# A graph attention kernel: node projection ahead of edge counting, and 84 ring tiles gathered while the edges are counted

## Chip, cores and metric

The kernel runs on one core of one Trainium2 chip. The metric is the device time of one execution in microseconds. Before the change it is 3249.47 us, the median of 3 runs (3248.05 to 3252.27).

## What is computed

3125 nodes with 256 features and 50000 edges sorted by destination go through four layers, each added to its input: two graph attention layers, a mixture of experts, a five-hop graph convolution, and attention over slices. The change lies in the first stages of the graph layers. Of the reference that part is:

```python
hx = (x @ Wg).reshape(n, h, f)
he = (ea @ Wge).reshape(-1, h, f)
al = jax.nn.leaky_relu(einsum(hx, a_s)[src] + einsum(hx, a_d)[dst] + einsum(he, a_e), 0.2)
...
out = jax.ops.segment_sum(hx[src] * al[:, :, None], dst, num_segments=n)
```

Further on, the convolution sums `norm[:, None] * h[col]` over the edges five times. The kernel does that as a product with a dense matrix that holds, for each pair of nodes, how many edges join them. This matrix is what "counting the edges" means.

## The kernel before, in words

The edges are padded to 50176 and lie in 392 tiles of 128. The nodes are 25 blocks of 128. The program is a chain of stages. Each stage gives every engine its own list of instructions, and a barrier of all engines stands between two stages, so a stage ends when its last engine is done. The stages around the change are, in their order before:

- **Tables** (`graph_tables`): degrees, segment ends and the edge terms.
- **Counting** (`counts`, lines 944 to 1019, with the class `Counter`): 67 of the 131 windows of the count matrix. A window is three tiles of edges and one of overlap. Per window VectorE (DVE) writes a one-hot `dst_hot` (line 807) and three one-hots `src_hot` (line 812) in float16, TensorE (PE) multiplies them (line 845), ScalarE (ACT) copies the sum out (line 822) to one of three buffers, and SyncE (SP) stores it (line 830). After the windows DVE works out one "item" of a slow path for odd graphs (`AnyOrder`, lines 898 to 920). GpSimd (POOL) stores this item with an indirect DMA (line 928). It first waits for the semaphore `ready`, loads the number of items into a register (line 876), enters a loop, and waits for the item itself.
- **Projection** (`project_nodes`): `hx = x @ Wg` and the node terms, block by block, stored as rows of 260 floats in the DRAM tensor `hx_rows` (line 419).
- **Lookup** (`lookup`, lines 659 to 773): for each edge the source's terms, through one-hots and PE products. DVE multiplies by a mask (line 749) and reduces (line 733), 98 groups of four tiles. In each of the 14 chunks of seven groups it also makes one wide one-hot (line 725) and one mask (line 727).
- **Edge weights** (`edge_weights`): segment sums and maxima with scans, and 32 more counting windows beside them.
- **Aggregation** (`aggregate`): the rows gathered per edge are weighted and summed per node.

The rows per edge come from `Gather.on_gpsimd` (line 637): POOL issues one indirect DMA (line 645) per tile of 128 edges, which reads 128 rows of `hx_rows` into one slot of a ring of 112 tiles in SBUF. A counter of pairs of tiles says how far it may run ahead. In the first layer `AHEAD` is 56 pairs everywhere, so all 112 tiles of the ring are gathered in the lookup, and the next 280 wait in the aggregation until a slot is free. In the second layer 34 pairs are gathered in the lookup, and the rest of the ring in the edge weights.

The instructions of POOL stand in one queue per stage. In the lookup they are an iota (line 704), the clearing of the edge table (line 706), and then the gathers.

Of the kernel before, what the change touches and what calls it, by code (L numbers as in the profile page):

```python
# [43 lines left out]
def after(count):  # L44


    return count + 1


class Linked:  # L50


    def __init__(self, eng, sem, base=0):
        self.eng, self.sem, self.base, self.n = eng, sem, base, 0
# [7 lines left out]
class Space:  # L62
# [20 lines left out]
    def sb(self, name, shape, dt=F32):  # L83
        return self.ctx.enter_context(self.nc.sbuf_tensor(f"{self.tag}_{name}", shape, dt))
# [20 lines left out]
def across(row, width):  # L105

    return row.rearrange("(a n) -> a n", a=1).to_broadcast([P, width])
# [514 lines left out]
class Gather:  # L622

    AHEAD = ((56, 56, 56, 56), (34, 42, 46, 56))

    def __init__(self, nc, ctx, g, layer):
        s = Space(nc, ctx, f"gat{layer}")
        self.g, self.sent = g, 0  # L630
        self.upto = self.AHEAD[layer]
        self.ring = s.sb("ring", [P, RING, ROW])
# [311 lines left out]
def counts(nc, g, io):  # L944

    with ExitStack() as ctx:
        s = Space(nc, ctx, "cnt1")
        c = g.counter
        anyhow = AnyOrder(s, g)
        part, keys, lasts, numbers = (s.sb(n, [P, ET]) for n in ("part", "keys", "lasts", "numbers"))  # L950
        last_i = s.sb("last_i", [P, ET], I32)
        wide, long = s.sb("wide", [P, WINDOWS]), s.sb("long", [P, WINDOWS - 1])
        whole = [s.ps(f"acc{i}", (P, c.BANKS, 512)) for i in range(3)]
        apart = s.ps("apart", (P, c.BANKS, 512))
        numbered, linked, ready, given = (s.sem(n) for n in ("numbered", "linked", "ready", "given"))
        windows = range(c.MAIN)
        full = WINDOWS - 1
        with s.block() as block:
            @block.sync
            def _(sp):  # L960
                sp.dma_start(last_i[:, :], across(io["tile_last"], ET)).then_inc(given, 16)
                for j in windows:
                    c.store(sp, j)
                c.all_stored(sp, c.MAIN)

            @block.gpsimd
            def _(pool):
                pool.iota(c.number[:, :], pattern=[[1, QUARTER]], base=0, channel_multiplier=0,
                          allow_small_or_imprecise_dtypes=True).then_inc(numbered, 1)
                pool.iota(numbers[:, :], pattern=[[1, ET]], base=0, channel_multiplier=0,  # L970
                          allow_small_or_imprecise_dtypes=True).then_inc(numbered, 1)
                pool.iota(anyhow.lane[:, :], pattern=[[0, 1]], base=0, channel_multiplier=1).then_inc(numbered, 1)
                pool.wait_ge(ready, after(1))
                anyhow.on_gpsimd(pool)

            @block.vector
            def _(dve):
                link = Linked(dve, linked)
                column = c.column[:, :]
                link(dve.tensor_copy(c.count16[:, :], g.count[:, :]))  # L980
                link(dve.tensor_copy(column, g.src_i[:, :]))
                link(dve.tensor_scalar(part[:, :], column, float(QUARTER), None, ALU.is_ge))
                for q in (2, 3):
                    link(dve.scalar_tensor_tensor(part[:, :], column, float(q * QUARTER), part[:, :], ALU.is_ge, ALU.add))
                link(dve.scalar_tensor_tensor(column, part[:, :], float(-QUARTER), column, ALU.mult, ALU.add))
                link(dve.scalar_tensor_tensor(keys[:, :], g.dst_f[:, :], 4.0, part[:, :], ALU.mult, ALU.add))
                dve.wait_ge(given, after(16))
                link(dve.tensor_copy(lasts[:, :], last_i[:, :]))
                link(dve.memset(g.first4[:, 0:1], 0.0))
                link(dve.tensor_scalar(g.first4[:, 1:WINDOWS], lasts[:, TRIPLE - 1:ET - 1:TRIPLE], 4.0, 4.0, ALU.mult, ALU.add))  # L990
                link(dve.memset(g.first4[:, WINDOWS:], 4.0 * (N + 2)))
                base = g.first4[:, 0:full]
                link(dve.tensor_tensor(c.key[:, 0:full, 0:TRIPLE], keys[:, 0:TRIPLE * full].rearrange("p (j i) -> p j i", i=TRIPLE),
                                       base.unsqueeze(2).to_broadcast([P, full, TRIPLE]), ALU.subtract))
                link(dve.tensor_tensor(c.key[:, 0:full, TRIPLE], keys[:, TRIPLE:ET:TRIPLE], base, ALU.subtract))
                link(dve.tensor_tensor(c.key[:, full, 0:ET - TRIPLE * full], keys[:, TRIPLE * full:],
                                       g.first4[:, full:full + 1].to_broadcast([P, ET - TRIPLE * full]), ALU.subtract))
                dve.wait_ge(numbered, after(3))
                c.on_vector(dve, windows)
                link(dve.tensor_tensor(wide[:, :], g.first4[:, 1:], g.first4[:, 0:WINDOWS], ALU.subtract))  # L1000
                link(dve.tensor_scalar(wide[:, :], wide[:, :], float(4 * SPAN), None, ALU.is_gt))
                link(dve.tensor_tensor(long[:, :], lasts[:, TRIPLE:ET:TRIPLE], lasts[:, TRIPLE - 1:ET - 1:TRIPLE], ALU.is_equal))
                link(dve.tensor_tensor(wide[:, 0:full], wide[:, 0:full], long[:, :], ALU.add))
                link(dve.tensor_reduce(g.odd[:, :], wide[:, :], AX, ALU.max))
                link(dve.tensor_scalar(g.odd[:, :], g.odd[:, :], 1.0, None, ALU.min))
                link(dve.tensor_scalar(anyhow.items[:, :], g.odd[:, :], float(anyhow.ITEMS - 1), 1.0, ALU.mult, ALU.add))
                link(dve.memset(lasts[:, ET - 1:ET], float(NP - 1)))
                dve.sem_inc(ready, 1)
                anyhow.on_vector(dve, link, c, numbers, keys, lasts, apart)

            @block.scalar
            def _(act):
                c.on_scalar(act, windows, whole, False)

            @block.tensor
            def _(pe):
                c.on_tensor(pe, windows, whole)
                pe.wait_ge(ready, after(1))
                anyhow.on_tensor(pe, apart)
# [1462 lines left out]
def main_program(nc, io, out):  # L2482
    with ExitStack() as whole:
        g = Space(nc, whole, "all")
# [18 lines left out]
        with ExitStack() as graph:  # L2503
            sb = lambda n, shape, dt=F32: graph.enter_context(nc.sbuf_tensor(n, shape, dt))
            g.src_i, g.dst_f = sb("src_i", [P, ET], I32), sb("dst_f", [P, ET])
            g.indeg, g.inv_deg, g.has = (sb(n, [P, NB]) for n in ("indeg", "inv_deg", "has"))
            g.seg_start, g.seg_end = sb("seg_start", [P, NB], I32), sb("seg_end", [P, NB], I32)
            g.tiles, g.tile_quads = sb("tiles", [P, NB + 1], I32), sb("tile_quads", [P, NB + 1], I32)
            g.small_sb = sb("small_sb", [P, NB, SW])
            g.block_first = sb("block_first", [P, NB])  # L2510
            g.node_d, g.w_self = sb("node_d", [P, NB, 4]), sb("w_self", [P, NB, 4])
            graph_tables(nc, g, io)
            g.counter = Counter(nc, graph, g)
            counts(nc, g, io)
            project_nodes(nc, g, io, 0, io["x"], True)
            for layer, target in enumerate((g.x_mid, g.x_gnn)):
                if layer:
                    project_nodes(nc, g, io, layer, g.x_mid, False)
                with ExitStack() as held:

                    words = ET * SW + 2 * NB * SW
                    room = held.enter_context(nc.sbuf_tensor(f"room{layer}", [P, words], F32))
                    g.per_edge = room[:, 0:ET * SW].rearrange("p (j c) -> p j c", c=SW)
                    g.spare = room[:, ET * SW:ET * SW + 2 * NB * SW].rearrange("p (n b c) -> p n b c", n=2, c=SW)
                    g.gather = Gather(nc, held, g, layer)
                    lookup(nc, g, layer)
                    g.w_cols = held.enter_context(nc.sbuf_tensor(f"w_cols{layer}", [P, ET, 4], F32))
                    edge_weights(nc, g, io, layer)
                    aggregate(nc, g, io, layer, target)
# [40 lines left out]
```

## Time and profile before

| what | value |
|---|---|
| median of 3 runs | 3249.47 us |
| the profiled execution's own time | 3252.93 us |
| its span | 3251.1 us |
| counting, 153.5 to 288.7 us of the span | 135.2 us |
| projection, 288.7 to 362.9 us | 74.2 us |
| lookup, 362.9 to 531.4 us | 168.5 us |
| busy in the span: PE, DVE, ACT, POOL | 70%, 55%, 29%, 33% |

The stage bounds are the first instruction of a stage on any engine, read from the timeline. The busy shares are means over all stages and say nothing on a single one. In each stage the question is which engine reaches the barrier last. A timeline row gives the start, the length, the engine, the line and the operation, with the idle time ahead of it and what released it in brackets. Neighbouring instructions of one kind are merged into one row with their count.

### The profile page before, as it was taken

The page shows a single profiled execution, that of the slowest core. Times are in us where ns is not written, and L with a number is a line of the kernel's source. Part 1 is how long each engine was busy: PE and PEld are TensorE (multiplying, and loading weights), DVE is VectorE, ACT ScalarE, POOL GpSimd, SP SyncE. Part 2 cuts the span into 40 slices and gives each one's busy share as a digit, 9 for nine tenths or more (in the row PEclk, how much of TensorE's full clock was granted, in tenths as well). Part 3 has the DMA queues.
Part 4 walks back from the last instruction along what each step waited for, and adds up shares of the span by engine and source line. Part 5 has one row for each costly group of instructions (what it writes and reads, how often), then busy time and mean ns, then how long its engine had stood idle before and what let it go on. Part 6 is the DMA issues. An engine that isn't in the chain of part 4 may idle for free. (4 is left out here: it accounts for less than half of the span.)

```text
span 3251.1 us, 40675 instructions
## 1 busy us (share of the span) xinstructions
PE 2271.6 (70%) x11685; PEld 1667.0 (51%) x11685; DVE 1777.6 (55%) x4118; ACT 941.5 (29%) x1613; POOL 1056.9 (33%) x1034
## 2 busy tenths in 40 slices
PE   5394662628766554537887489915999999996767
PEld 1142452216544343215565367704888888884446
DVE  6497698657744357637775310058444444435643
ACT  5352100301100010210000012217666666662321
POOL 0000472717777526757777433030000000000000
PEclk9797886859987876769998689957999999998987
DMA  4133552324444345435555489343555565640001
GB/s 168 15 124 115 179 179 68 99 68 117 122 115 113 103 169 177 129 104 157 161 165 155 130 303 379 139 129 91 142 151 143 144 150 142 152 112 10 0 14 42
DMA packets 367972, 420.74 MB, mean 129 GB/s; under 512 B 47984, under 2 KB 325585, under 8 KB 364599
## 3 DMA queue, kind: packets, MB, share of 16 engines
q1 hardware_dynamic: 271530, 220.90, 22.8%
q0 software_dynamic: 50496, 151.73, 16.2%
q10 hardware_dynamic: 45792, 46.27, 4.3%
q8 instruction: 72, 1.18, 0.2%
q14 instruction: 82, 0.66, 0.1%
HBM read 329.39 MB, written 90.23 MB: 129 GB/s over the span
## 5 line engine op out<-in xcount | busy, mean ns | idle before, releaser
L645 POOL DMA_INDIRECT gat_ring<-hx_rows,src_i x784 | 820.4, 1046 | 335.8 <-issue 233.4
L2150 PE MATMUL hop_sums<-hop_pieces,hop_weights 128*128 128x512 f32 x3125 | 712.6, 390 | 107.4 <-DVE hop_pieces L2053 107.4
L2150 PEld LDWEIGHTS hop_sums<-hop_pieces,hop_weights 128*128 128x128 f32 x3125 | 588.7, 188 | 231.3 <-DVE hop_pieces L2053 109.1
L2088 ACT ACTIVATE hop_weights<-hop_columns 128x640 fp32r<-128x640 f16 x625 | 459.8, 739 | 221.5 <-PE hop_sums L2150 207.5
L1614 PE MATMUL agg_acc<-agg_msg,agg_oh 128*128 x976 | 275.5, 434 | 120.7 <-DVE agg_oh L1526 120.5
L1614 PE MATMUL agg_acc<-gat_ring,agg_oh 128*128 x976 | 261.7, 411 | 71.0 <-DVE agg_oh L1523 68.5
L1614 PEld LDWEIGHTS agg_acc<-agg_msg,agg_oh 128*128 128x128 f32 x976 | 197.1, 212 | 194.5 <-issue 161.7
L1614 PEld LDWEIGHTS agg_acc<-gat_ring,agg_oh 128*128 128x128 f32 x976 | 178.0, 198 | 149.8 <-issue 129.8
L2203 POOL IOTA slc_valid<- 128x25 f32 x1 | 0.2, 163 | 757.3 <-POOLq L76 757.3
L1523 DVE TENSOR_SCALAR agg_oh<-agg_nodes,dst_f,w_cols 128x128 f32<-128x128 f32 x488 | 174.8, 405 | 121.6 <-PE agg_acc L1614 61.1
L770 PE MATMUL look_bank<-look_pieces,look_part 128*128 128x125 bf16 (+1 forms) x2352 | 149.1, 232 | 101.6 <-DVE look_part L725 52.3
L1509 DVE TENSOR_TENSOR agg_msg<-gat_ring,w_cols (+1 forms) x98 | 121.7, 1242 | 131.7 <-SPq L656 109.1
L770 PEld LDWEIGHTS look_bank<-look_pieces,look_part 128*128 128x128 f16 x2352 | 131.1, 114 | 120.0 <-DVE look_part L749 57.2
L2067 DVE TENSOR_SCALAR hop_h<-hop_sums,all_dis 128x256 f32<-128x256 f32 x125 | 60.5, 484 | 230.7 <-PE hop_sums L2150 230.5
L822 ACT ACTIVATE cnt_out<-wts_acc 128x800 f16<-128x800 f32 x64 | 53.6, 837 | 398.3 <-PE wts_acc L845 395.2
L812 DVE TENSOR_SCALAR cnt_src_hot<-cnt_number,cnt_column 128x800 f16<-128x800 f16 x392 | 144.3, 420 | 1.9 <-PE wts_acc L845 1.5
L845 PE MATMUL wts_acc<-cnt_src_hot,cnt_dst_hot 128*128 128x400 f16 x508 | 101.4, 353 | 59.9 <-DVE cnt_src_hot L812 56.4
L845 PE MATMUL cnt_acc<-cnt_src_hot,cnt_dst_hot 128*128 128x400 f16 x536 | 103.2, 338 | 47.8 <-DVE cnt_src_hot L812 42.6
L1871 DVE TENSOR_TENSOR exp_y<-exp_down,exp_b 128x256 f32<-128x256 f32 x32 | 11.3, 416 | 225.2 <-PE exp_down L1922 225.2
L1908 PE MATMUL exp_up<-exp_xt,exp_w 128*128 128x512 f32 x256 | 124.2, 613 | 6.6 <-ACT exp_xt L1881 6.6
L1922 PE MATMUL exp_down<-exp_w,exp_hid 128*128 128x256 f32 x512 | 119.6, 379 | 0.0
L1526 DVE TENSOR_TENSOR agg_oh<-agg_nodes,dst_f 128x256 f32<-128x256 f32 x244 | 96.5, 419 | 38.7 <-PE agg_acc L1614 35.0
(447 smaller groups left out, 3029.9 us busy)
## 6 DMA issues: line engine op xcount, KB each, us to landing
hop_columns<-count_rows SPq DMA_DIRECT2D x60, 1600.0 KB, 8.0
look_part<-src_low SPq DMA_DIRECT2D x28, 896.0 KB, 5.3
exp_w<-in_L_ffn_w SPq DMA_DIRECT2D x16, 1024.0 KB, 15.5
count_windows<-cnt_out SPq DMA_DIRECT2D x67, 200.0 KB, 1.9
count_windows<-cnt_out ACTq DMA_DIRECT2D x64, 200.0 KB, 1.9
gat_ring<-hx_rows,src_i POOLq DMA_INDIRECT x784, 2.8
hx_rows<-prj_row SPq DMA_DIRECT2D x50, 130.0 KB, 1.9
agg_own<-hx_rows ACTq DMA_DIRECT2D x50, 130.0 KB, 2.6
```

Source lines behind the costliest of these rows:

```text
L645: pool.indirect_dma_start(out=self.ring[:, t % RING, :], out_offset=None, in_=self.g.hx_rows, in_offset=bass.IndirectOffsetOnAxis(ap=self. ...
L770: mm = pe.matmul(bank[n % BANKS][:, k * WIDE:(k + 1) * WIDE], hot[c % 2][:, j * P:(j + 1) * P], pieces[:, piece, :], start=(piece == 0), s ...
L812: made = dve.tensor_scalar(self.src_hot[:, t % self.SRC, :], self.number[:, :], self.column[:, t:t + 1], None, ALU.is_equal)
L845: mm = pe.matmul(whole[j % sets][:, n, 0:self.COLS], self.dst_hot[:, j % self.HOT, i, :], self.src_hot[:, t % self.SRC, n * self.COLS:(n + ...
L1509: weighted = dve.tensor_tensor(at(msg, q % 2).rearrange("p (k f) -> p k f", f=F + 1), at(ring, q % HELD).rearrange("p (k f) -> p k f", f=F ...
L1523: hot = dve.tensor_scalar(oh[k][:, n, :], nodes[b % 2], at(g.dst_f, tile), at(g.w_cols, tile)[:, 0:1], ALU.is_equal, ALU.mult)
L1526: hot = dve.tensor_tensor(oh[k][:, :, :], nodes[b % 2].unsqueeze(1).to_broadcast([P, 2, P]), g.dst_f[:, bass.ds(4 * q + 2 * k, 2)].unsquee ...
L1614: mm = pe.matmul(sums, oh[k][:, n, :], moving[:, t:t + R], start=False, stop=False, skip_group_check=True)
L1908: mm = pe.matmul(up[c % 2][:, :], w1[i][:, k, c:FF:KF], xt[:, k, :], start=(k == 0), stop=(k == 1))
L1922: mm = pe.matmul(down[q][:, 0:D], hid[c % 2][:, q * P:(q + 1) * P], w2[i][:, c, :], start=(c == 0), stop=(c == KF - 1), skip_group_check=True)
L2088: act.activation(weights[:, q % SLOTS_W, :, :], columns[n % STAGES][:, c * GROUP:(c + 1) * GROUP, b % 2 * P:(b % 2 + 1) * P], ACT.Copy).th ...
L2150: mm = pe.matmul(sums[m % BANKS][:, :], weights[:, q % SLOTS_W, i, :], pieces[k % 2][:, t, :], start=(t == 0), stop=(t == NB - 1))
```

## The change

The call of `counts` moves behind the projection of the first layer, to a place where the ring exists. In it, POOL gathers 42 pairs, which are 84 of the ring's 112 tiles, after its three iotas and ahead of its wait for `ready`. The lookup then asks for 56 pairs as before, so that 28 tiles are left to it. Nothing else is edited.

```diff
     AHEAD = ((56, 56, 56, 56), (34, 42, 46, 56))
+    WHILE_COUNTING = 42
...
                 pool.iota(anyhow.lane[:, :], pattern=[[0, 1]], base=0, channel_multiplier=1).then_inc(numbered, 1)
+                g.gather.on_gpsimd(pool, g.gather.WHILE_COUNTING)
                 pool.wait_ge(ready, after(1))
                 anyhow.on_gpsimd(pool)
...
             g.counter = Counter(nc, graph, g)
-            counts(nc, g, io)
             project_nodes(nc, g, io, 0, io["x"], True)
...
                     g.gather = Gather(nc, held, g, layer)
+                    if not layer:
+                        counts(nc, g, io)
                     lookup(nc, g, layer)
```

On POOL, counting and lookup before (`cnt_...` are counting's tiles, `gat_ring` is the ring, `room` holds the edge table; TENSOR_LOAD is the load of the number of items, and the DMA to `count_rows` the store of the item):

```order
L968 IOTA cnt_number 128x800
L970 IOTA cnt_numbers 128x392
L972 IOTA cnt_lane 128x1
L876 TENSOR_LOAD cnt_items
L928 DMA count_rows<-cnt_item_out,cnt_item_rows 12800x800
L704 IOTA look_lane 128x1
L706 MEMSET room 128x3136
L645 DMA gat_ring<-hx_rows,src_i 128x260 x112
```

And now:

```order
L969 IOTA cnt_number 128x800
L971 IOTA cnt_numbers 128x392
L973 IOTA cnt_lane 128x1
L646 DMA gat_ring<-hx_rows,src_i 128x260 x84
L877 TENSOR_LOAD cnt_items
L929 DMA count_rows<-cnt_item_out,cnt_item_rows 12800x800
L705 IOTA look_lane 128x1
L707 MEMSET room 128x3136
L646 DMA gat_ring<-hx_rows,src_i 128x260 x28
```

84 gathers stand ahead of the load of the item count and of the item's store. 28 of the 112 stay where they were.

On SP's queue, from counting to the lookup before (`prj_x` and `prj_w` are the projection's input and weights, `look_part` the lookup's):

```order
L961 DMA cnt_last_i<-in_tile_last 128x392
L830 DMA count_windows<-cnt_out 128x800 x67
L311 DMA prj_x<-in_x 128x5x256 x5
L409 DMA prj_w<-in_L_gnn_Wg 128x2x256
L695 DMA look_part<-src_high 128x392
L699 DMA look_part<-src_low 128x3584 x14
```

And now:

```order
L311 DMA prj_x<-in_x 128x5x256 x5
L409 DMA prj_w<-in_L_gnn_Wg 128x2x256
L962 DMA cnt_last_i<-in_tile_last 128x392
L831 DMA count_windows<-cnt_out 128x800 x67
L696 DMA look_part<-src_high 128x392
L700 DMA look_part<-src_low 128x3584 x14
```

The two stages have changed places, and each has the same transfers as before.

## Rows read from the trace of the kernel before

**Rows 1.** Windows: stretches inside counting, its end, the projection's end, the lookup, its end.

```profile
core 0: us, PE busy (x) PEld busy (x) DVE busy (x) ACT busy (x) POOL busy (x), PEclk, DMA share, GB/s
200.00:220.00 20.00, 18.94 (x102) 8.78 (x100) 20.00 (x51) 10.51 (x13) 0.00 (x0) 1.00 0.34 128
340.00:363.00 23.00, 14.17 (x62) 9.26 (x60) 9.08 (x35) 5.27 (x12) 0.02 (x1) 0.94 0.38 127
372.00:516.00 144.00, 96.87 (x1122) 81.71 (x1119) 133.54 (x203) 0.00 (x0) 111.10 (x109) 0.80 0.56 176
```

**Rows 2.** Timeline of POOL: first, an ordinary and last of the lookup's 112 gathers.

```profile
366.04 0.99 POOL L645 DMA_INDIRECT gat_ring<-hx_rows,src_i  x1 [0.16 <-issue]
...
376.39 0.94 POOL L645 DMA_INDIRECT gat_ring<-hx_rows,src_i  x1 [0.30 <-issue]
377.64 0.94 POOL L645 DMA_INDIRECT gat_ring<-hx_rows,src_i  x1 [0.30 <-issue]
...
515.14 0.95 POOL L645 DMA_INDIRECT gat_ring<-hx_rows,src_i  x1 [0.30 <-issue]
```

**Rows 3.** Timeline of DVE: lookup groups beside gathers, after them, and the last one.

```profile
504.50 0.68 DVE L749 TENSOR_TENSOR look_part<-look_bank,look_part 128x500 f32<-128x500 f32 x1
...
505.89 0.68 DVE L749 TENSOR_TENSOR look_part<-look_bank,look_part 128x500 f32<-128x500 f32 x1
...
518.67 0.68 DVE L749 TENSOR_TENSOR look_part<-look_bank,look_part 128x500 f32<-128x500 f32 x1
...
520.07 0.68 DVE L749 TENSOR_TENSOR look_part<-look_bank,look_part 128x500 f32<-128x500 f32 x1
...
527.63 1.25 DVE L733 TENSOR_REDUCE room<-look_part 128x20 f32<-128x500 f32 x2
```

**Rows 4.** Timeline of counting: POOL's last iota, first window, and what follows the last window.

```profile
154.78 0.30 POOL L972 IOTA cnt_lane<- 128x1 int32 x1
...
160.09 0.69 DVE L807 TENSOR_TENSOR cnt_dst_hot<-cnt_count,cnt_key 128x512 f16<-128x512 f16 x1
...
268.99 0.28 DVE L1000 TENSOR_TENSOR cnt_wide<-all_first 128x131 f32<-128x131 f32 x1
```

**Rows 5.** Timeline of DVE: two neighbouring windows of counting, POOL idle.

```profile
201.16 0.68 DVE L807 TENSOR_TENSOR cnt_dst_hot<-cnt_count,cnt_key 128x512 f16<-128x512 f16 x1
201.76 1.10 DVE L812 TENSOR_SCALAR cnt_src_hot<-cnt_number,cnt_column 128x800 f16<-128x800 f16 x3
202.77 0.68 DVE L807 TENSOR_TENSOR cnt_dst_hot<-cnt_count,cnt_key 128x512 f16<-128x512 f16 x1
```

**Rows 6.** Timeline of POOL, second layer's edge weights: indirect DMAs while DVE makes counting windows.

```profile
1316.86 1.41 POOL L645 DMA_INDIRECT gat_ring<-hx_rows,src_i  x1 [0.30 <-issue]
1318.57 1.31 POOL L645 DMA_INDIRECT gat_ring<-hx_rows,src_i  x1 [0.30 <-issue]
1320.19 1.30 POOL L645 DMA_INDIRECT gat_ring<-hx_rows,src_i  x1 [0.30 <-issue]
1321.80 1.46 POOL L645 DMA_INDIRECT gat_ring<-hx_rows,src_i  x1 [0.30 <-issue]
...
1324.82 0.98 POOL L1156 DMA_INDIRECT room<-edge_scan,seg_end  x1 [0.30 <-issue]
1326.11 0.98 POOL L1156 DMA_INDIRECT room<-edge_scan,seg_end  x1 [0.30 <-issue]
```

**Rows 7.** Timeline of DVE at that place: two windows beside POOL's indirect DMAs.

```profile
1330.43 0.68 DVE L807 TENSOR_TENSOR cnt_dst_hot<-cnt_count,cnt_key 128x512 f16<-128x512 f16 x1
...
1332.04 0.68 DVE L807 TENSOR_TENSOR cnt_dst_hot<-cnt_count,cnt_key 128x512 f16<-128x512 f16 x1
```

**Rows 8.** Timeline of the end of counting, up to the next stage's first instruction.

```profile
273.04 0.72 DVE L887 MEMSET cnt_total<- 128x800 f32 x1 [0.23 <-DVE cnt_own L886]
274.87 0.42 DVE L898 TENSOR_SCALAR cnt_pick<-cnt_numbers,cnt_tile 128x392 f32<-128x392 f32 x1 [1.10 <-issue]
...
281.69 0.16 DVE L914 SCALAR_TENSOR_TENSOR cnt_item_rows<-cnt_window,cnt_row 128x1 int32<-128x1 f32 x1
...
282.77 1.15 POOL L928 DMA_INDIRECT count_rows<-cnt_item_out,cnt_item_rows  x1 [127.69 <-DVE cnt_item_rows L914]
288.76 4.42 SPq L311 DMA_DIRECT2D prj_x<-in_x  x5
```

**Rows 9.** Instructions on the tile cnt_out in counting: ACT's copies, SP's stores, landing.

```profile
L822 ACT ACTIVATE cnt_out<-cnt_acc x67: 837/837/838, 165.1 to 270.7; 128x800 f16<-128x800 f32 x67
L830 SPq DMA_DIRECT2D count_windows<-cnt_out x67: 319/320/342, 165.9 to 271.6; - x67
...
DMA to landing us min/median/max: 1.9/1.9/2.6
```

**Rows 10.** Instructions of line 645 in the lookup: the landing of its gathers.

```profile
DMA to landing us min/median/max: 2.7/2.8/6.1
```

## The prediction

> **What bounds the kernel now.** The stages are cut apart by barriers, so I read each touched stage for the engine that arrives last, and only then the change.
>
> First the windows by stage [rows 1]. In a stretch inside counting DVE is busy for all of its 20.00 us and POOL for none. In the lookup DVE is busy 133.54 of 144 us and POOL 111.10. In the projection's last stretch neither is full. So DVE is the suspect in counting and in the lookup, and POOL a second one in the lookup.
>
> Second, the lookup's timeline, to see who comes last. POOL's first gather starts at 366.04 and its 112th ends at 515.14 + 0.95 = 516.1 [rows 2]. DVE's last reduction ends at 527.63 + 1.25 = 528.9 [rows 3]. The gathers are therefore over 12.8 us before the stage is. They are also not in DVE's way: one group takes 505.89 - 504.50 = 1.39 us beside gathers and 520.07 - 518.67 = 1.40 us after the last one [rows 3]. The 112 gathers cost this stage nothing that I can see.
>
> Third, the end of counting. DVE's last window is done at 268.99 [rows 4]. The item's arithmetic follows; POOL, which has waited 127.69 us, issues the item's store at 282.77, 0.92 us after DVE's step at 281.69 + 0.16, and the next stage's first transfer is issued at 288.76 [rows 8]. SP's last store was issued at 271.6 and lands in 2.6 us at most [rows 9]. So POOL's store ends this stage: whatever delays POOL at 282.77 delays the program.
>
> **The change part by part.** *The swap of stages.* Projection and counting use nothing of each other. Each keeps its instructions and transfers, and each still begins with PE idle. I cost the swap at nothing; a microsecond either way at the boundaries goes into the range.
>
> *84 gathers out of the lookup.* They take 84 x (0.94 + 0.30) us off POOL there, and none off the stage, since DVE ends it and its beat is the same with and without them [rows 3]. I cost this at 0. If the cover were gone, that is if POOL ended the stage, the gain would be at most the time that DVE doesn't need, and here that is below zero. Nothing downstream gains either: the aggregation finds the ring full in both kernels, and its 280 further gathers wait for freed slots.
>
> *84 gathers into counting.* POOL is idle there, but the gathers stand ahead of the item's store in the same queue. So the question is whether 84 of them end before 281.85, when DVE hands the item over.
>
> Their pace is not the lookup's. Alone a gather starts every 1.25 us (377.64 - 376.39, [rows 2]). While DVE makes counting windows, four gathers started at 1316.86, 1318.57, 1320.19 and 1321.80, and took 1.30 to 1.46 us in place of 0.94 [rows 6]: mostly 1.61 us from start to start. That is the beat of the windows themselves, 202.77 - 201.16 = 1.61 us [rows 5]: one gather for each window. DVE pays nothing for it. Its window is 1332.04 - 1330.43 = 1.61 us beside POOL as well [rows 7].
>
> Here a page bears on it, and it speaks against this change. The Trainium skill, "SBUF — State Buffer", section "SBUF: two separate sides", says that DVE and GpSimd have one port pair in common, which whoever starts first holds for the whole instruction, and that a DMA issued from GpSimd can't have its descriptors written while a DVE instruction in a fast mode holds it. By that a gather would get on only in the windows' other part. The rows agree that POOL is held up beside these windows, and show no DVE instruction held up by a gather; the rule taken to its end is a rival below.
>
> Now the sum, on the profile's own clock.
> - POOL's last iota ends at 154.78 + 0.30 = 155.08 [rows 4]; with the 0.16 us ahead of the lookup's first gather [rows 2] the first starts at 155.24. Four start before the first window at 160.09 (155.24 + 3 x 1.25 = 158.99).
> - The fifth starts at 160.24. From there to 268.99 is 108.75 us, or 67.3 beats of 1.615. That gives 68 starts, the last at 268.45. Now 72 are issued, and POOL is free about 270.0 (1.31 + 0.30 later).
> - 12 are left, at 1.25 us: 15.0 us, the last one over at 284.7. In this stretch DVE still runs a few float16 and float32 one-hots and copies, such as the 0.72 and 0.42 us in [rows 8]; I add 1 us for them: 285.7.
> - Then POOL loads the item count and enters its loop. Before, this lay under its wait. DVE's own load and entry show as 1.10 us between 273.76 and 274.87 [rows 8]; POOL's I take as the same, and the 0.92 us up to the store as before. The store is issued at 285.7 + 1.1 + 0.9 = 287.7.
> - It was issued at 282.77. Late by 4.9 us, call it **+5 us**, all on the path, since the next stage follows this store.
>
> The bounds. Below: if no gather were held up, 84 x 1.25 = 105 us would end at 260.2, before the item is ready, and the change would cost 0. Above: if the beat of 1.615 held through the tail too, 84 x 1.615 = 135.7 us would end at 290.9, and the store would start at 292.9: +10. I take the middle case because the rows nearest to it, gathers of this very line beside these very windows, show one per window, and after the windows such instructions return to 0.94 us.
>
> The profiled execution took 3252.93 us, 3.5 above the median. 3252.93 + 5.0 - 3.5 = **3254.5 us**: 0.15% slower, inside the 0.2% (6.5 us) that a measurement of this kernel can tell from no change.
>
> **The rivals.**
>
> *POOL is in time.* The lock to the beat is not strict: at 1324.82 and 1326.11 two indirect DMAs passed in 0.98 us each, beside windows [rows 6], after DVE had paused. If every third gather goes like that, the 68 starts in the windows become some 75, four more gathers (5 us) are saved and the item is waited for again: +0 to +2 us, **3250.5 us**. For it: those rows. Against: [rows 6] also shows the beat taken up at once. Chance 0.18.
>
> *POOL is later.* The DVE work after the windows holds up gathers as the windows do, and the tail runs at 1.615: +10 us, **3259.5 us**. It decides from +6.5 us on, that is from a tail pace of about 1.4 us. For it: the item's arithmetic has such instructions. Against: they fill a small part of those 13 us. Chance 0.17.
>
> *The stores become the wait.* Stores already take 0.34 of the DMA engines in counting [rows 1]. Gathers of 133 KB each 1.61 us come on top. ACT copies into three buffers, so a buffer must come back within three beats, 4.84 us: 0.84 for the copy, 0.32 for the issue, and the landing, 1.9 us now [rows 9]. From a landing of about 3.6 us on, ACT, then PE, then DVE wait; each further microsecond costs 67 / 3 = 22 us. At 4.6 us: **3272 us**. For it: gathers in the lookup took up to 6.1 us to land [rows 10]. Against: the lookup moved 176 GB/s at a share of 0.56 [rows 1], and such landings were single ones. Chance 0.06.
>
> *The port is held to the end.* If a gather's 0.94 us had to fit into the 0.6 us of a window that is not `src_hot`, each would need two windows, 3.2 us. By 269 only 4 + 34 would be issued, 46 would be left, 57.5 us, the store at about 329: +46 us, **3296 us**. That is what the page's rule would give, taken strictly. Against: [rows 6] has one per window. Chance 0.03.
>
> *The lookup gains.* Faster needs DVE or its loads in the lookup to be slowed by gathers in a way that the beat of [rows 3] doesn't show. To pass 0.2% it must be 6.5 us, over 0.06 us on each of 98 groups, where I see 0.01. Price at that point: **3243 us**. Chance 0.06.
>
> **How the numbers follow.** The forecast, POOL late by 2 to 6.5 us, has 0.50; with "in time" (0.18) the same within 0.2% is 0.68. Slower is "later", "stores" and "port": 0.17 + 0.06 + 0.03 = 0.26. Faster is 0.06. The range of 8 in 10 takes in the three cases that differ by POOL's pace alone: from 0 less a boundary's 2 us to +10 and 1.5 us of scatter: 3247.5 to 3261.
>
> **What the changed profile would show.** The lookup as long as before, 166 to 169 us from its first instruction to the next stage's, with DVE's groups at 1.39 us, and POOL there done after 28 gathers. In counting, gathers of about 1.31 us, one per window; windows at 1.61 us; 70 to 74 gathers begun when the windows end; the item's store some 18 to 19 us after that in place of 13.8, and released by no wait for DVE. A store that still follows DVE's step by 0.92 us would show POOL in time. Windows longer than 1.61 us, with ACT waiting for landings, would show the stores. I would be wrong on the main point if counting and projection together grew by nothing while the lookup got shorter.

## The result, and the profile after

| | median us | runs | range us |
|---|---|---|---|
| before | 3252.08 | 10 | 3247.57 to 3255.57 |
| after | 3258.66 | 10 | 3255.62 to 3261.38 |

The ratio is 1.0023, with a 95% interval of 1.0013 to 1.0033. The change costs 6.6 us between the medians: slower, clear of no change, and at about the 0.2% that I had set as the line. The profiled execution after has a span of 3259.3 us (before 3251.1).

In the changed kernel the projection runs from 153.6 to 227.87 us of the span, counting to 370.60, and the lookup to 538.14. So the projection takes 74.2 us as before, counting 142.7 in place of 135.2, and the lookup 167.5 in place of 168.5. The two changed stages give +7.5 and -1.0, together +6.5, which is the difference of the medians. The two profiled executions differ by 8.2 us; the other 1.5 us lie behind the lookup, where the kernels are the same.

Windows of the changed kernel: inside counting, inside the lookup, and between the two (columns as in [rows 1]).

```profile
274.00:294.00 20.00, 18.95 (x102) 8.75 (x101) 20.00 (x51) 10.41 (x13) 16.35 (x13) 1.00 0.68 209
380.00:524.00 144.00, 97.97 (x1123) 82.99 (x1122) 133.50 (x203) 0.00 (x0) 23.76 (x24) 0.80 0.27 96
...
361.50:370.50 9.00, 0.00 (x0) 0.00 (x0) 0.00 (x0) 0.00 (x0) 0.00 (x0) 0.50 0.00 0
```

The first two answer to [rows 1]. In counting POOL is now busy for 16.35 of 20 us, and DVE makes the same 51 instructions in the same time. In the lookup POOL is almost empty, and DVE is as busy as before: 133.50 us. The third line is new. For 9 us no engine computes and no DMA engine moves a byte.

The timeline of POOL in the changed kernel: the first gather, two in step with the windows, the last two of that kind and the first after, the last, the item's store, and the lookup's first instruction.

```profile
229.39 1.11 POOL L646 DMA_INDIRECT gat_ring<-hx_rows,src_i  x1
...
242.94 1.31 POOL L646 DMA_INDIRECT gat_ring<-hx_rows,src_i  x1 [0.30 <-issue]
244.55 1.31 POOL L646 DMA_INDIRECT gat_ring<-hx_rows,src_i  x1 [0.30 <-issue]
...
343.08 1.31 POOL L646 DMA_INDIRECT gat_ring<-hx_rows,src_i  x1 [0.30 <-issue]
344.70 0.95 POOL L646 DMA_INDIRECT gat_ring<-hx_rows,src_i  x1 [0.30 <-issue]
...
357.84 0.95 POOL L646 DMA_INDIRECT gat_ring<-hx_rows,src_i  x1 [0.30 <-DVE cnt_item_rows L915]
359.09 1.01 POOL L929 DMA_INDIRECT count_rows<-cnt_item_out,cnt_item_rows  x1 [0.30 <-issue]
370.63 0.14 POOL L705 IOTA look_lane<- 128x1 f32 x1 [10.52 <-ACTq L693]
```

The gathers go as [rows 6] had them, one per window. The item's store follows the last gather at once. (The bracket of the last gather names DVE's item. In POOL's list that wait stands behind the gathers and ahead of the store, so the gather itself did not need it.) Then POOL seems to do nothing for 10.52 us.

The timeline of DVE in the changed kernel: two windows, the first step behind the windows, the hand-over of the item, counting's last step, the lookup's first, two groups of the lookup beside gathers, and its end.

```profile
273.44 0.67 DVE L808 TENSOR_TENSOR cnt_dst_hot<-cnt_count,cnt_key 128x512 f16<-128x512 f16 x1
...
275.06 0.67 DVE L808 TENSOR_TENSOR cnt_dst_hot<-cnt_count,cnt_key 128x512 f16<-128x512 f16 x1
...
344.50 0.28 DVE L1002 TENSOR_TENSOR cnt_wide<-all_first 128x131 f32<-128x131 f32 x1
...
357.45 0.16 DVE L915 SCALAR_TENSOR_TENSOR cnt_item_rows<-cnt_window,cnt_row 128x1 int32<-128x1 f32 x1
...
358.28 0.16 DVE L921 TENSOR_TENSOR cnt_tile<-cnt_tile,cnt_keep 128x1 f32<-128x1 f32 x1
370.64 0.25 DVE L713 COPY look_value<-small_sb 128x100 f32<-128x100 f32 x1 [12.20 <-PEq L76]
...
401.89 0.67 DVE L750 TENSOR_TENSOR look_part<-look_bank,look_part 128x500 f32<-128x500 f32 x1
...
403.28 0.68 DVE L750 TENSOR_TENSOR look_part<-look_bank,look_part 128x500 f32<-128x500 f32 x1
...
534.48 1.25 DVE L734 TENSOR_REDUCE room<-look_part 128x20 f32<-128x500 f32 x2
```

A window still takes 1.62 us [rows 5, 7] and a group of the lookup 1.39 [rows 3]. DVE is done with counting at 358.44 and then waits 12.20 us for the barrier.

What POOL does in that time is not among the busy instructions. It stands in its queue, under the line of the stage's block, where each engine issues a DRAIN ahead of the barrier. A row gives the length in ns (least, median, greatest) and the start. Counting's block in the changed kernel:

```profile
L959 DVEq DRAIN  x1: 17/17/17, 358.7 to 358.7; - x1
L959 POOLq DRAIN  x1: 7000/7000/7000, 362.0 to 362.0; - x1
```

The same in the kernel before:

```profile
L958 DVEq DRAIN  x1: 10/10/10, 282.9 to 282.9; - x1
L958 POOLq DRAIN  x1: 136/136/136, 285.8 to 285.8; - x1
```

POOL's drain has grown from 0.136 to 7.000 us, and it is the last thing ahead of the barrier. Before, the gathers had this drain in the lookup, where DVE came later. The lookup's block before (two layers; the first starts are the first layer's):

```profile
L692 POOLq DRAIN  x2: 20602/22870/25139, 500.2 to 1276.5; - x2
...
L692 DVEq DRAIN  x2: 10/10/10, 529.1 to 1281.0; - x2
```

In the first layer POOL's drain ended at 500.2 + 25.1 = 525.3, which is 9.2 us after the last gather's end at 516.1 [rows 2], and still 3.8 us ahead of DVE at 529.1. (POOL's queue runs ahead of the recorded spans, so a drain's row can begin while gathers are still running, as here at 500.2; its end is what counts.) In the second layer, where 68 gathers stand in the lookup, the same line has POOL's drain ending at 1276.5 + 20.6 = 1297.1, 16 us after DVE's at 1281.0. There gathers and drain end the stage already in the kernel before.

### The profile page after: what moved, and what is told of

Its sections match the earlier page's. It is cut to its first block and busy times, and to the rows that moved or that the text cites. A ratio compares the mean times of both kernels' runs of the same rounds, so it can differ in the third digit from the quotient of the medians.

```text
span 3259.3 us, 40667 instructions
## 1 busy us (share of the span) xinstructions
PE 2277.5 (70%) x11685; PEld 1672.3 (51%) x11685; DVE 1779.8 (55%) x4118; ACT 941.6 (29%) x1613; POOL 1077.1 (33%) x1034
## 5 line engine op out<-in xcount | busy, mean ns | idle before, releaser
L646 POOL DMA_INDIRECT gat_ring<-hx_rows,src_i x784 | 841.0, 1073 | 334.8 <-issue 231.1
```

The source lines that it names most:

```text
L646: pool.indirect_dma_start(out=self.ring[:, t % RING, :], out_offset=None, in_=self.g.hx_rows, in_offset=bass.IndirectOffsetOnAxis(ap=self. ...
```

## The experiments

The theories. **Order**: the swap of the stages costs the time, by its boundaries. **Backlog**: the drain waits for what the last gathers left behind; it goes if POOL has time between them and the block's end. **Fixed**: the drain costs a set time for each indirect DMA, whatever POOL waits for in between. I held the second to be likeliest.

### The swap alone (e1)

```diff
-    WHILE_COUNTING = 42
+    WHILE_COUNTING = 0
```

> The swap of the two stages alone: no tile is gathered while edges are counted, all 112 in the lookup. Theory 'backlog' (POOL's drain at the end of a stage waits for work of the indirect DMAs that no row shows as busy; it took 7.0 us in counting after the change and 0.14 us before): the drain is 0.1 to 0.3 us again, the item is stored 129 us after counting's first instruction as before, and the time is that of the kernel before within 1.5 us. Theory 'order' (the extra time lies in going from counting straight to the lookup): still 5 to 7 us slower than before.

Measured: 3251.11 us beside 3252.02 of before, ratio 0.9997 (0.9988 to 1.0007). The drain is back at its old length:

```profile
L959 POOLq DRAIN  x1: 136/136/136, 360.3 to 360.3; - x1
```

The swap is neutral. "Order" falls, and all of the cost is the gathers'.

### 72 tiles in place of 84 (e2)

```diff
-    WHILE_COUNTING = 42
+    WHILE_COUNTING = 36
```

> 36 pairs (72 tiles) in place of 42 while edges are counted; the last gather should end about 115 to 116 us after counting's first instruction, some 14 us before the item is handed over. 'Backlog': those 14 us are enough to work off a backlog of 8 to 9 us, the drain is under 1 us, and the time is from 0.5 us below to 2.5 us above the kernel before (what DVE lost in the stage, 1.5 us, may stay). 'Order': 5 to 7 us slower. 'Fixed' (a stage with gathers ends in a drain of some 0.08 us per gather, whenever they were issued): the drain is about 6 us and the time 5 to 7 us above the kernel before.

Measured: 3256.47 us, ratio 1.0016 (1.0007 to 1.0025). POOL's item store and the drain in this kernel, from the timeline and from the block's line:

```profile
358.49 1.01 POOL L929 DMA_INDIRECT count_rows<-cnt_item_out,cnt_item_rows  x1 [15.44 <-DVE cnt_item_rows L915]
```

```profile
L959 POOLq DRAIN  x1: 6020/6020/6020, 361.4 to 361.4; - x1
```

POOL now stood idle for 15.44 us before the item, so that it is late for nothing. The drain is 6.02 us all the same. What the gathers had left behind would have been gone in 15 us: "backlog" falls, and with it the theory that I had begun with.

### The item made late (e3)

84 tiles, and 13 more clearings of a buffer on DVE ahead of the item, each chained to the last:

```diff
-        link(dve.memset(self.total[:, :, :], 0.0))
+        for _ in range(14):
+            link(dve.memset(self.total[:, :, :], 0.0))
```

> The changed kernel with 13 more clearings of one tile on DVE, about 10 to 11 us, between the windows and the item; POOL's list is untouched. 'Backlog': the item is stored some 10 to 11 us later, but the drain behind it falls from 7.0 us to under 1 us, so the kernel is only 3 to 5 us slower than the changed one (10 to 12 us above the kernel before). 'Fixed': the drain stays at 7 us and the whole delay is paid: 10 to 11 us slower than the changed kernel (17 us above the kernel before).

Measured: 3270.14 us, ratio 1.0056 (1.004 to 1.0071). POOL waits 12.53 us for the item, and the drain does not shrink:

```profile
L960 POOLq DRAIN  x1: 7000/7000/7000, 373.7 to 373.7; - x1
```

It is the same 7.000 us with a wait ahead of it and without. That is "fixed", to the nanosecond.

### All 112 tiles while counting (e4)

```diff
-    WHILE_COUNTING = 42
+    WHILE_COUNTING = 56
```

> All 112 tiles while edges are counted, none in the lookup. By every theory the item waits for 28 more gathers at 1.25 us, 35 us, and the stage pays them: 40 to 46 us above the kernel before. 'Backlog': the drain is 8 to 11 us, as at the end of a run of 112 gathers in the lookup before (9.2 us from the last row to the end of the drain). The lookup now runs without a gather: by my prediction it takes 167 to 168.5 us as ever; if gathers slowed it, by the rival, it would be 3 us or more shorter.

Measured: 3297.76 us, ratio 1.0143 (1.0128 to 1.0159). POOL is late by its whole surplus: the item's store starts at 393.43, 36.6 us behind the start of DVE's hand-over at 356.80. The drain:

```profile
L959 POOLq DRAIN  x1: 9287/9287/9287, 396.4 to 396.4; - x1
```

0, 72, 84 and 112 gathers give 0.136, 6.020, 7.000 and 9.287 us. Each of the three is 0.136 + 0.0817 for every gather. And the lookup without a single gather beside it takes 165.2 us from its first instruction to its barrier, where with all 112 it takes 165.7 (e1) and 166.3 (the kernel before). The gathers cost DVE there about a microsecond at most, in its wait for the low halves (`src_low`): 0.5 us here, 1.3 in e1 and 1.8 before.

### 72 tiles, drained early (e5)

If the drain counts the indirect DMAs since the last drain, one more drain under POOL's 15 us wait must take the cost off the path:

```diff
                 g.gather.on_gpsimd(pool, g.gather.WHILE_COUNTING)
+                pool.drain()
                 pool.wait_ge(ready, after(1))
```

> As with 72 tiles, plus one explicit drain of POOL right behind the gathers of counting, ahead of its wait for the item. The drains measured so far are 0.136 us for the item alone, 6.020 for 72 gathers more, 7.000 for 84, 9.287 for 112: 0.0817 us per indirect DMA issued since the last drain, and 12 us of idle time did not shorten it. Theory 'per DMA since the last drain': the explicit drain takes about 5.9 us within the 15 us for which POOL waits anyway, the stage's own drain is 0.14 us again, and the kernel is 4 to 6 us faster than without it: from 1.5 us below to 1.5 us above the kernel before. Theory 'per DMA of the stage' (the work is done only at the stage's end, however often one drains): the stage's drain stays at 6 us and the time 4 to 5 us above the kernel before.

Measured: 3250.61 us beside 3251.74 of before, ratio 0.9997 (0.9989 to 1.0006). POOL's last gather and its store of the item, then the added drain (line 975) and the block's:

```profile
340.39 1.31 POOL L646 DMA_INDIRECT gat_ring<-hx_rows,src_i  x1 [0.30 <-issue]
357.15 1.01 POOL L929 DMA_INDIRECT count_rows<-cnt_item_out,cnt_item_rows  x1 [15.45 <-DVE cnt_item_rows L915]
```

```profile
L975 POOLq DRAIN  x1: 25295/25295/25295, 322.3 to 322.3; - x1
```

```profile
L959 POOLq DRAIN  x1: 144/144/144, 360.1 to 360.1; - x1
```

The early drain ends at 347.6, some 5.9 us after the last gather's end at 341.7, and POOL waits for the item until 357.15. The block's drain is back at 0.144 us, and 5.9 us of e2 are gone. One instruction shows it: this drain was the cost. What is left is a kernel as fast as before with 72 gathers out of the lookup, and with nothing that makes use of it.

### The lookup's masks on POOL (e6, e7)

POOL is now free in the lookup, and DVE bounds it. So the first layer's 14 masks (0.88 us each on DVE, 12.3 us) go to POOL, as a difference and a test for zero. POOL makes mask c as soon as its buffer is free, that is when DVE has multiplied the last group of chunk c - 2, and issues up to four gathers ahead of it. e6 does this on top of e5. e7 does it without gathers in counting and without the added drain, with all 112 gathers in the lookup, up to eight ahead of a mask.

```diff
+                    for c in range(CHUNKS):
+                        if c >= 2:
+                            gather.on_gpsimd(pool, max(gather.sent, min(upto, gather.sent + gather.PER_CHUNK)))
+                            pool.wait_ge(multed, after((c - 1) * PER))
+                        make_mask(pool, c)
```

> The kernel with 72 tiles and the early drain, and in the first lookup the 14 masks (DVE, 0.88 us each) made by POOL in two instructions each, a difference and a comparison with zero, in the time that the moved gathers left. Theory 'DVE bounds the lookup': 14 x 0.88 = 12.3 us less in the lookup, 10 to 13 us below the kernel before. Rival 'port': POOL's two instructions hold the port pair against DVE's wide one-hots, or come too late for DVE, and the gain is under 5 us or a loss.

> The same masks on POOL, but with all 112 gathers left in the lookup (swap of stages only). POOL then has 112 x 1.25 = 140 us of gathers, 3 us of set-up, 14 masks of 2 to 4 us and a drain of 9.2 us, 180 to 208 us in all against some 154 us of DVE: POOL ends the lookup, and the kernel is 10 to 40 us slower than the kernel before. Were gathers and masks no rivals for POOL's time, it would be as fast as the one with 72 tiles moved.

Measured: e6 3254.01 us, ratio 1.0005 (0.9996 to 1.0014); e7 3298.57 us, ratio 1.0143 (1.0128 to 1.0158). e7 says that the masks need the gathers out of the way: with both, POOL ends the lookup 18.7 us after DVE, and DVE waits 20.8 us for masks. But e6 gained nothing either. The costliest groups of DVE in the lookup show why. First e5 (columns: busy us, mean ns of one, idle before):

```profile
L726 DVE TENSOR_SCALAR look_part<-look_part,look_lane 128x3584 f16<-128x3584 f16 x14 | 16.2, 1155 | 1.1 <-DMA look_part<-src_low 1.1
L728 DVE TENSOR_TENSOR look_part<-all_count,look_part 128x700 f16<-128x700 f32 x14 | 12.3, 878 | 0.0
```

Then e6:

```profile
L749 DVE TENSOR_SCALAR look_part<-look_part,look_lane 128x3584 f16<-128x3584 f16 x14 | 26.8, 1921 | 0.0
```

The masks' 12.3 us are gone from DVE, and the wide float16 one-hot has grown from 1.155 to 1.921 us, 14 times: 10.7 us given back. Two of DVE's first small steps, beside the first mask, give back the rest: a cast takes 1.37 us in place of 0.23, a difference 0.90 in place of 0.29. Where mask and one-hot meet, on the timelines of POOL and DVE in e6:

```profile
427.90 1.39 POOL L702 TENSOR_TENSOR look_part<-all_count,look_part 128x700 f16<-128x700 f32 x1 [2.25 <-DVE look_part L771]
429.38 2.69 POOL L706 TENSOR_SCALAR look_part<-look_part 128x700 f16<-128x700 f16 x1
```

```profile
428.31 1.93 DVE L749 TENSOR_SCALAR look_part<-look_part,look_lane 128x3584 f16<-128x3584 f16 x1
```

POOL's difference starts 0.41 us ahead of the one-hot. The one-hot ends 0.95 us after it, and POOL's second step ends 1.83 us after the one-hot. That reads as if each stood until the other was done. The 98 groups in float32, which run beside the masks too, keep their 0.677 us. This is what the Trainium skill, "SBUF — State Buffer", section "SBUF: two separate sides", says of a DVE instruction in a two-port mode and GpSimd: whoever starts first keeps the shared ports for the whole instruction. The order of starts and ends above agrees with it; that the one-hot is in such a mode no run here shows.

### The masks two groups later (e8)

The remedy is to start the mask behind the one-hot:

```diff
-                            pool.wait_ge(multed, after((c - 1) * PER))
+                            pool.wait_ge(multed, after((c - 1) * PER + 2))
```

> 72 tiles, early drain and the first lookup's masks on POOL as in the run with masks on POOL, but each mask from the third on waits for two more groups of VectorE, so that it no longer begins just ahead of VectorE's float16 one-hot. Theory 'collision': the masks brought nothing because POOL's mask starts 0.4 us before that one-hot (427.90 against 428.31 in the run before this) and the one-hot then takes 1.93 us in place of 1.15: 14 x 0.78 = 10.8 us given back of the 14 x 0.88 = 12.3 us saved. Then the one-hot is back at about 1.15 us, the lookup is 10 to 12 us shorter than in the run without masks on POOL, and the kernel takes 3238 to 3241 us: ratio 0.996 to 0.997. Rival 'share': POOL's elementwise work slows VectorE wherever it runs, and the float32 groups of 0.68 us pay for it in place of the one-hot: 4 groups per chunk, each longer by some 0.2 us, 11 us in all, and the kernel stays at 3250 to 3255 us. Rival 'late': POOL, with 4.1 us of mask and up to four gathers per chunk, has its mask ready after the chunk begins; VectorE then waits on POOL and the time is 3255 us or more.

Measured: 3243.89 us beside 3250.79 of before, ratio 0.9977 (0.9966 to 0.9987). The one-hot in the groups of DVE:

```profile
L749 DVE TENSOR_SCALAR look_part<-look_part,look_lane 128x3584 f16<-128x3584 f16 x14 | 17.5, 1255 | 0.0
```

It is back at 1.255 us, the groups stay at 0.678, and the lookup takes 156.9 us up to its barrier in place of 165.7 (e5). "Collision" holds, and "share" and "late" fall. The lookup is 8.8 us shorter where I expected 10 to 12, and the time is 2.9 us above my range. The first chunks explain most of the lookup's part: the first two masks still meet DVE's first steps. The cast and the difference stay as slow as in e6, 1.7 us together, and the one-hots, two of them still slow, are 1.4 us above e5. That leaves 9.2 of the 12.3 us.

### The edge table cleared by ScalarE (e9)

In the kernel before, the lookup's start shows the same collision. POOL, then DVE:

```profile
363.07 2.81 POOL L706 MEMSET room<- 128x3136 f32 x1
```

```profile
362.98 0.25 DVE L712 COPY look_value<-small_sb 128x100 f32<-128x100 f32 x1 [3.21 <-PEq L76]
...
363.27 2.65 DVE L713 COPY look_value<-small_sb 128x25 f32<-128x25 f32 x1
```

A copy of a quarter of the size takes ten times as long beside the memset. ScalarE idles in this stage, so on top of e8 it clears the table (a finite tensor times zero), in both layers:

```diff
-                pool.memset(g.per_edge[:, :, :], 0.0).then_inc(numbered, 1)
...
+            @block.scalar
+            def _(act):
+                act.activation(g.per_edge[:, :, :], g.count[:, 0:SW].unsqueeze(1).to_broadcast([P, ET, SW]), ACT.Copy,
+                               scale=0.0).then_inc(numbered, 1)
```

> The run with shifted masks, and the edge table of both lookups cleared by ScalarE, which does nothing in that stage, in place of POOL's memset. Theory 'collision': the same contention costs DVE at the lookup's start, where its copy of 128 x 25 takes 2.65 us beside POOL's memset of 2.82 us (362.62 and 362.42 in the run before this) and its copy of 128 x 100, just ahead of it, 0.25 us. Without the memset that copy takes about 0.2 us, the first layer's lookup is 1 to 2.5 us shorter (its low halves still have to land), and the second layer's, where POOL comes last, is shorter by POOL's 2.7 us: in all 3.5 to 5 us, so 3239 to 3241 us beside 3250.8 of before, ratio 0.996 to 0.997. Rival 'own': the copy of 128 x 25 is slow by itself, because of its source's stride; then it stays at 2.65 us, the first lookup gains nothing, the second 2.7 us, and the time is 3241 to 3242 us.

Measured: 3239.62 us beside 3251.63 of before, ratio 0.9964 (0.9951 to 0.9978): 12 us faster than the kernel before, and the best of the study. The timeline of ACT and DVE:

```profile
363.59 2.82 ACT L781 ACTIVATE room<-all_count 128x3136 f32<-128x3136 f32 x1 [15.98 <-PEq L76]
...
363.90 0.18 DVE L736 COPY look_value<-small_sb 128x25 f32<-128x25 f32 x1
```

The copy takes 0.18 us beside an equally long clearing on ScalarE. So it was POOL's, and "own" falls. The first layer's lookup becomes 0.9 us shorter (DVE then waits for the low halves), the second's 2.1 us, where POOL comes last.

## Why the prediction was right, and where it was not

The number held: 3254.5 predicted, 3258.66 measured, inside the range, slower as the sum said. Of the 4.2 us between the two, 2.6 are the base: 3252.08 from ten runs, where I had 3249.47 from three. By the number alone the rival "POOL is later" (3259.5) is nearer, but not by its mechanism: the last 11 gathers took 14.1 us, 1.28 each, and not 1.615. My own mechanism was only half right.

- **The swap costs nothing**: right (e1).
- **84 gathers out of the lookup save nothing**: right. The stage went from 168.5 to 167.5 us with the beat of [rows 3] unchanged. "The lookup gains" falls.
- **One gather per window**: right. 73 gathers had begun when the windows ended (72 predicted), and 11 were left; the last was over at 358.79, 130.9 us after the stage's start, where the prediction had 285.7 - 153.6 = 132.1. "The port is held to the end" falls for gathers beside these windows, and "the stores become the wait" too: stores now land in 1.9 us at the least, 2.0 at the median and 3.7 at most (before 1.9, 1.9 and 2.6 [rows 9]), and the windows keep their beat.
- **"Then POOL loads the item count and enters its loop"**, 1.1 + 0.9 us: this term failed. The store begins 0.30 us after the last gather. The register work of this loop stands in POOL's queue at 347.5 us, under the gathers; the queue runs ahead of them.
- **"Late by 4.9 us"**: mis-sized. Counted from the stage's first instruction the store was issued after 131.2 us in place of 129.2: 2.0 us late. Of these only 0.5 us are POOL's, since DVE's own hand-over came after 129.6 us in place of 128.1. Of DVE's delay, 1.0 us is one wait for PE among the windows, which the kernel before does not have. That is no effect of the gathers that I can show: the hand-over came after 128.5 us in e1, with none, and with 72 after 128.6 in e5 and 129.3 in e2. So on this point the rival "POOL is in time" was nearer.
- **"All on the path, since the next stage follows this store"**: this is the step that failed. I read the next stage's start as a fixed distance from the store. What stands between them is POOL's drain, and it grows with the gathers moved: 7.000 - 0.136 = 6.9 us. There was even a sign of it in [rows 2, 3]: the gathers end 12.8 us before DVE, and I took all of that as cover without asking what POOL does behind its last gather.

The sum on the profiles is then: store 2.0 later, drain 6.9 longer, and 1.2 less between the drain's end and the next stage's first instruction (2.8 before, 1.6 after; 1.6 in e1 too), which is +7.7 beside the +7.5 of counting, less 1.0 of the lookup. The term "POOL late" was 4.4 us too large by its own mechanism, and the drain, 6.9 us, was missing. The two errors cancelled in large part, so the right range is partly luck. e2 shows this most plainly: there POOL is in time with 15 us to spare, and by my steps the cost should have been nil; it was 4.5 us, and a drain at another place (e5) takes it away.

## What to carry to other kernels

An indirect DMA leaves a debt that its engine pays at the next drain, 0.08 us for each one here, so moving many of them into another stage moves that debt in front of another barrier. Look at the DRAIN rows of each queue under a block's line, not only at the last busy instruction, and where the engine waits anyway, drain there. Work taken off an engine gains only when something of use takes its place, and here elementwise work on GpSimd paid only once it no longer started just ahead of VectorE's wide float16 instruction.

## What I had not expected of the hardware

- POOL's drain behind indirect DMAs is exact at the end of counting: 0.136, 6.020, 7.000 and 9.287 us for 0, 72, 84 and 112 gathers, the same with 0 or 12.5 us of waiting ahead of it. During the 7.000 us no DMA engine moves anything, so it is not the landing of data. In the lookup it is not always exact. From the last gather's end to the drain's end, 112 gathers take 9.2 us (by the rate 9.3) and the second layer's 68 take 5.6 (5.7), but the 28 of the changed kernel take 3.1 (2.4), and 40 take 4.7 in e5 and 5.1 in e2 (3.4). All gathers here read 128 rows, so a price per gather and one per row are not told apart. What POOL does in this time the traces do not show, and it stays open.
- The two engines hold each other up in both directions: the one-hot on DVE 1.155 to 1.921 us, the test for zero on POOL 2.69 us beside it and 1.97 behind it (e8), a small copy on DVE 0.18 to 2.65 us beside a memset. The gathers' way beside counting's windows is gentler: 0.95 to 1.31 us, and DVE's windows keep their 1.62.
